# Groups of two tokens instead of four in a recurrence, with row statistics made one stage earlier

## The reference

```python
def step(h, bu_t):
    Wh = jnp.fft.ifft(lambdas * jnp.fft.fft(h)).real
    h_new = Wh + bu_t
    return (h_new, h_new)
...
y = jnp.einsum('sbn,dn->bsd', hs, C_w) + D * u
...
x = x + 0.5 * _L0_ffn_ref(_layernorm(x, axis=-1), L0_ffn_gate_w, L0_ffn_w1, L0_ffn_w2)
x = x + _L0_attn_ref(_layernorm(x, axis=-1), L0_attn_a_params, L0_attn_B_w, L0_attn_C_w, L0_attn_D)
x = x + 0.5 * _L0_ffn_ref(_layernorm(x, axis=-1), L0_ffn_gate_w, L0_ffn_w1, L0_ffn_w2)
```

## Time and profile before

| | us |
|---|---|
| median of 3 runs | 150.54 |
| lowest and highest run | 150.45, 153.68 |
| the profiled execution's own time | 150.5 |
| its span in the trace | 148.6 |
| PE busy | 128.5 (86%) |
| DVE busy | 88.2 (59%) |
| ACT busy | 56.1 (38%) |
| POOL busy | 56.0 (38%) |

### The profile page before, as it was taken

One profiled execution on the slowest core, in us unless ns is written; L12 is line 12 of the kernel. 1 busy time (PEld: TensorE's weight loads), 2 busy tenths in 40 slices (PEclk: granted clock), 3 DMA queues, 4 the chain that ended last, 5 costly groups with the idle time before them and its releaser, 6 DMA issues.

```text
span 148.6 us, 2493 instructions
## 1 busy us (share of the span) xinstructions
PE 128.5 (86%) x749; PEld 96.6 (65%) x749; DVE 88.2 (59%) x379; ACT 56.1 (38%) x156; POOL 56.0 (38%) x96
## 2 busy tenths in 40 slices
PE   5988989699799989379999999999989969999920
PEld 2315334289699965137887788778976249999810
DVE  1198787994467431257679668988894133755310
ACT  2522434235353302055756675752010035553200
POOL 3490002777205778001212211231100677665570
PEclk9999999999999999999999999999995599999995
DMA  4999995236660111690013441344024312211110
GB/s 89 305 351 401 350 290 144 55 108 185 194 203 22 57 53 53 213 321 35 2 45 101 146 133 39 123 148 146 0 76 158 91 46 56 56 38 40 43 45 18
DMA packets 15740, 18.49 MB, mean 124 GB/s; under 512 B 1904, under 2 KB 10608, under 8 KB 15600
## 3 DMA queue, kind: packets, MB, share of 16 engines
q1 hardware_dynamic: 13936, 15.34, 32.7%
q0 software_dynamic: 1280, 2.66, 6.3%
q10 hardware_dynamic: 512, 0.34, 0.9%
HBM read 12.70 MB, written 7.73 MB: 138 GB/s over the span
## 4 chain that ended last, share of the span: by engine, by line
PE 46%; DMA 14%; issue 10%; ACT 9%; POOL 7%; DVE 5%; SPq 4%; POOLq 1%
PE pair L1062 9%; PE pair L1075 9%; ACT u L520 7%; DMA w1s<-w 5%; PE pair L1158 5%; POOL xg L370 5%; PE pair L1149 4%; SPq L292 3%; PE pair L1180 3%; PE pair L1182 3%; PE pair L943 2%; DMA xg<-x,tok 2%; DMA x<-x_scratch 2%; DMA xg<-x_scratch,tok 2%; PE pair L1087 2%
## 5 line engine op out<-in xcount | busy, mean ns | idle before, releaser
L943 PE MATMUL pair<-warm_in,ones_bf 128*128 128x512 bf16 x61 | 18.9, 457 | 3.9 <-DMA x<-x_scratch 2.3
L1062 PE MATMUL pair<-xcT,w1s 128*128 128x160 f32 x128 | 20.5, 303 | 0.6 <-ACT xcT L452 0.6
L1062 PEld LDWEIGHTS pair<-xcT,w1s 128*128 128x128 f32 x128 | 18.0, 190 | 1.7 <-ACT xcT L452 1.7
L460 ACT ACTIVATE hT<-pair 128x320 f32<-128x320 f32 x32 | 13.8, 435 | 13.6 <-PE pair L1062 12.1
L1075 PE MATMUL pair<-hT,w2s 128*128 128x160 f32 x112 | 17.8, 302 | 0.0
L370 POOL DMA_INDIRECT xg<-x,tok x10 | 10.2, 1019 | 16.7 <-issue 16.7
L1075 PEld LDWEIGHTS pair<-hT,w2s 128*128 128x128 f32 x112 | 15.6, 190 | 0.0
L370 POOL DMA_INDIRECT xg<-x_scratch,tok x10 | 10.1, 1007 | 13.7 <-DMA x_scratch<-x 10.9
L943 PEld LDWEIGHTS pair<-warm_in,ones_bf 128*128 128x128 bf16 x61 | 6.8, 117 | 12.2 <-issue 4.1
L402 POOL TENSOR_TENSOR vb<-vq,st 128x128 f32<-128x128 f32 x8 | 3.8, 474 | 27.0 <-ACT vq L495 27.0
L381 POOL DMA_INDIRECT x_scratch<-xnew,tok x10 | 9.9, 985 | 10.3 <-DMA x_scratch<-x 7.6
(11 more groups left out here) (190 smaller groups left out, 242.8 us busy)
## 6 DMA issues: line engine op xcount, KB each, us to landing
x_scratch<-x SPq DMA_DIRECT2D x8, 272.0 KB, 2.1
...
```

Of the source, the lines that this page charges most:

```text
L460: nc.scalar.activation(hT[:, e % 2, half * HC:(half + 1) * HC, :], bank[4 + half][:, 0:HC * CAP] .rearrange("p (c s) -> p c s", c=HC), ACT ...
L943: M(bank[to][:, :], ones_bf[:, :], warm_in[:, :], start=True, stop=True)
L1062: ins = M(bank[4 + half][:, c * CAP:(c + 1) * CAP], w1s[:, i, ch * P:(ch + 1) * P], xcT[:, i * CAP:(i + 1) * CAP], start=True, stop=True)
```

## The change

- The recurrence works in groups of two tokens (`TR = 2`) and 256 groups a batch. `group_sums` becomes 2 matmuls of 256 columns that read `uT` with a stride; `vq`, `va`, `vb`, `z`, `zc`, `zs` are twice as wide; the part within a group becomes `within(i, 0)` and `within(i, 1)`, 2 matmuls and 432 columns each; the tables are smaller.
- POOL adds `state` for batches 0 to 6, DVE for batch 7.
- The mean and variance of `x`'s rows are made in the first expert stage. SP loads `x` into `x1` (`load_x`), DVE rates it (`rate_rows`, step `x`) into two more columns, and SP stores rows of 130 columns to `x1_scratch` (`store_x`). The rows of `xnew` are rated in step `o` as well, and a scatter waits for that. In the recurrence `stats` is gone, and `deviation` and `shift` are done for groups of batches (`RATED`).
- ACT's `normalise` is cut in halves on both sides of `turned_part`.
- The power levels 0 to 4 move from ahead of DVE's first gathered tile to between its steps `o`; levels 5 to 7 follow the last one.
- `x2` of batches 6 and 7 is added by PE and copied by ACT; `gate_back(6)` moves ahead of `carry(7)`. The `keep_warm` ahead of the recurrence has 10 matmuls instead of 14.

The core of the diff:

```diff
+    TR = 2
-    NG = SEQ // TB
+    NG = SEQ // TR
+    XP = D + 2
...
-        dve_steps = [steps("i0 i1 i2 i3 i4 d0 i5 i6 i7 i8 d1 i9 l0 f0 d2 "
-                         "o0 o1 d3 p5 o2 o3 d4 p6 o4 o5 d5 o6 d6 o7 o8 o9"),
+        dve_steps = [steps("i0 i1 i2 x0 i3 x1 i4 x2 d0 i5 x3 i6 x4 i7 x5 d1 i8 x6 i9 x7 l0 f0 d2 "
+                         "o0 o1 d3 p0 p1 o2 o3 d4 p2 p3 o4 o5 d5 p4 o6 d6 o7 o8 o9 p5 p6 p7"),
...
+            def load_x(b):
+                sp.dma_start(x1[:, b * TB:(b + 1) * TB, 0:D], tiles(x_rows, b)).then_inc(d_x1[b], 16)
+            def store_x(b):
+                sp.wait_ge(x_rated, b + 1)
+                sp.dma_start(tiles(x1_dram, b), x1[:, b * TB:(b + 1) * TB, :]).then_inc(d_fill, 16)
             for b in range(NB):
-                sp.wait_ge(d_gather[min(b + 3, NS - 1)], 16)
-                sp.dma_start(tiles(x1_dram, b), tiles(x_rows, b)).then_inc(d_fill, 16)
+                sp.wait_ge(d_gather[b], 16)
+                load_x(b)
+                if b >= 2:
+                    store_x(b - 2)
...
+                    if n == 0:
+                        pool.wait_ge(row_rated, j + 1)
...
+            def turn_forth(b):
+                pool.wait_ge(zs_r, b + 1)
+                pool.wait_ge(zc_r, b + 1)
+                if b >= 2:
+                    pool.wait_ge(y_ps, b - 1)
+                nc.gpsimd.tensor_tensor(state_out(b), by_group(zc), by_group(zs), ALU.add).then_inc(state_r, 1)
...
             for i in range(NB):
                 if i + 1 < NB:
                     copy_uT(i + 1)
+                if i == 1:
+                    deviation(3)
                 if i + 2 < NB:
-                    deviation(i + 2)
+                    normalise(i + 2, 0, TB // 2)
                 if i + 1 < NB:
                     turned_part(i + 1)
                 if i + 2 < NB:
-                    normalise(i + 2)
+                    normalise(i + 2, TB // 2, TB)
...
+                def rate_rows(b):
+                    dve.wait_ge(d_x1[b], 16)
+                    for t in range(b * TB, (b + 1) * TB):
+                        ins = V.bn_stats(sstat[:, t, :], x1[:, t, 0:D])
+                    link(ins)
+                    for t in range(b * TB, (b + 1) * TB):
+                        ins = V.bn_aggr(x1[:, t, D:XP], sstat[:, t, :])
+                    ins.then_inc(x_rated, 1)
...
+                        if n == 0:
+                            dve.wait_ge(row_sb, i + 1)
+                            link(V.bn_stats(nstat[:, i, :], xnew[:, i, 0:D]))
+                            V.bn_aggr(xnew[:, i, D:XP], nstat[:, i, :]).then_inc(row_rated, 1)
...
+                by_residue = uT[:, b % 2, :].rearrange("d (h r p) -> d r p h", h=2, r=TR)
+                for r in range(TR):
+                    ins = M(bank[5][:, 0:NG].rearrange("s (p h) -> s p h", h=2), vt[:, TR - 1 - r, :],
+                            by_residue[:, r, :, :], start=(r == 0), stop=(r == TR - 1))
...
+            def within(b, h):
+                if b >= 2 and h == 0:
+                    pe.wait_ge(x2_r, b - 1)
+                    pe.wait_ge(y_read, b - 1)
+                y = y_pair(b)
+                M(y[:, h, 0:TR * BLOCK], uT[:, b % 2, 2 * h * P:(2 * h + 1) * P], tab[:, :, :].rearrange("p r c -> p (r c)"),
+                  start=True, stop=False, skip_group_check=True)
+                ins = M(y[:, h, BLOCK:2 * BLOCK], uT[:, b % 2, (2 * h + 1) * P:(2 * h + 2) * P], tab[:, 0, :],
+                        start=False, stop=False, skip_group_check=True)
...
-            keep_warm(14, 7)
+            keep_warm(10, 7)
...
                 group_sums(i)
+                within(i, 0)
                 if i >= 1:
                     read_out(i - 1)
-                within_pairs(i)
                 turn_u(i + 1)
                 if i == NB // 2 + 2:
                     rank(1, 0)
-                within_rest(i)
+                within(i, 1)
```

More of the change, by code:

```diff
@@ L417, in _ @@
                 turn_cosine(i)
+                if i < LAST:
+                    turn_forth(i)
             gather(1)
@@ L860, in turn_forth @@
                     dve.wait_ge(y_ps, b - 1)
-                V.tensor_tensor(state[:, b % 2, :], zc[:, :], zs[:, :], ALU.add).then_inc(state_r, 1)
+                V.tensor_tensor(state_out(b), by_group(zc), by_group(zs), ALU.add).then_inc(state_r, 1)
             def add_back(b):
@@ L930, in _ @@
             encode_place(1, 1)
-            add_back(LAST - 1)
             index(1)
@@ L1233, in _ @@
                     rank(1, 0)
-                within_rest(i)
+                within(i, 1)
             group_sums(LAST)
+            within(LAST, 0)
             read_out(LAST - 1)
-            within_pairs(LAST)
             gates_within(LAST)
+            within(LAST, 1)
+            add_rows(LAST - 1)
             gates_carried(LAST)
-            within_rest(LAST)
             read_out(LAST)
```

265 lines of the change are left out of this document (123 added, 142 removed).

## The result

The changed kernel takes **163.1 us**, the median of 4 runs (160.74 to 163.43), beside 151.49 for the kernel before on the same chip (4 runs). The ratio is 1.071, 95% interval 1.045 to 1.096: slower, and outside the range given. The profiled execution of the changed kernel took 163.31 (span 161.4), that of before 150.5.

What follows compares the result with a forecast made beforehand. Bounds: PE and ACT taking turns in the recurrence, POOL's scatters in the first expert stage, then DVE there after the change. Sum: 150.5 + 2.6 (first stage) - 3.9 (recurrence) + 1.2 + 1.1 - 0.2 (end) = 151.3 us; range 148.3 to 155.5.

Steps and rivals of the forecast that it cites:

- the first expert stage: Gathers to last scatter: DVE becomes the bound through rating; last scatter starts at 60.6 instead of 57.15, 3.5 later.
- 4.7 late: Bound for the first expert stage if loads of x land 0.7 later each time (3.4) and DVE stalls once.
- Softmax to last scatter: First expert stage, from softmax start to the last scatter's start: 15.83 before, forecast 1.0 longer, with DVE the bound.
- less than DVE's own delay: First expert stage: g0 holds the third relu, so PE's fourth expert starts some 1.4 late, adding nothing to the sum.
- A fall of PE's clock in this stage: Sign of a wrong forecast: PE's granted clock falling in the first stage because of gaps between its steps o.
- over 90% busy from 31 to 60: Sign of a right forecast: DVE nearly full through the first expert stage.
- keep_warm: Ahead of turn_u(0): four fewer matmuls at 0.229 each give back 0.92.
- Recurrence: The seven gaps between turn_u starts shrink from 34.1 to 30.2, a gain of 3.9.
- The ring: Recurrence cycle over two batches: PE's within waits for gate_back of an earlier batch; 8.55 for two, 4.28 each.
- rival 3: Recurrence: group_sums' strided read of uT takes twice the time, +0.89 a batch, period 5.0, 156.3 us; chance 0.04.
- End of the recurrence: From turn_u(7) to the second stage's gather: +1.2 to va(7), +1.1 to gate_first, -0.2 before the gather.
- The slower rival: Over 153.5 us: doubled prices of wide operations give 154.5, late first-stage loads alone 152.5, both 155.7; chance 0.20.

Runs made afterwards that it cites:

- e3: The changed kernel with all eight loads of x issued at once ahead of the gathers, stores after them: 159.5 us, ratio 1.051.
- e11: The kernel before with only the change's loads and stores of x through SBUF, nothing rated: 153.9 us, ratio 1.011.
- e2: The kernel before with only the statistics and their traffic moved, groups of four, state on DVE: 159.0 us, ratio 1.055.
- e5: The changed kernel with group_sums reading uT in order and writing its sums strided: 160.9 us, ratio 1.065.
- e6: The changed kernel with the fourth expert's relu ahead of g0 in ACT's order: 158.7 us, ratio 1.050.
- e7: The changed kernel with 26 instead of 16 keep_warm matmuls ahead of the wait for the read back: 159.8 us, ratio 1.060.
- e12: The changed kernel with state added by DVE for every batch instead of by POOL: 160.3 us, ratio 1.055.
- e4: The changed kernel with power levels 0 to 4 again ahead of DVE's first gathered tile: 159.8 us, ratio 1.052.
- e9: The changed kernel with the edits of e3, e4, e5, e6 and e7 together: 155.2 us, ratio 1.020.
- e10: The kernel before with only x2 of batch 6 added by PE and copied by ACT: 151.2 us, ratio 1.000.
- e1: The changed kernel with the statistics, the traffic of x and the late power levels taken back: 162.8 us, ratio 1.078.

## Why the prediction was wrong, point by point

**The step that failed is the first expert stage**: "up to the softmax DVE has 8 x 1.19 + 7 x 0.42 + 2 copies of 0.25 = 12.9, and comes to `l0` at 43.8", with the third gather "near 27.80 + 2 x 1.3 = 30.4". Its prices were right (0.82 a step `o`, 0.75 to 0.82 a level against 0.87, 1.2 a batch), and so was the 12.9 of DVE's work (13.0 in e3); its mechanism, DVE bound by rating, was half of it. It took the transfers as free. What the runs show in its place: DVE starts that work at 32.16 and not at 30.4, and waits 2.9 for two loads in the middle of it, so the softmax starts at 48.42 (46.74 in the earliest execution of the same program) and not at 43.8. Of the late start 0.8 is a wrong reading: the earlier trace rows is the first gathered tile, the second comes 1.32 behind it, but the third lands at 31.24 in the kernel before already. In the profiles the added traffic alone moves the last scatter by 4.0 (e11), and with the rating by 7.2 (e2). The text did name late loads as a bound, "4.7 late" for the stage, with 0.7 more a load; they were 2 us more in the median (1.3 in e5, e6, e7 and e12) and 3.7 more for one. The 3.4 of the old copies, on the page of the kernel before, would have given that 0.7.

**Softmax to last scatter** was forecast 1.0 longer and is 2.7 longer. The moved levels, which were in the sum, cost 1.8 (e4); the lower clock, which was not, 1.3 (e6 and e3), and that is most of the 1.7 that are missing here. The two add up: e9, with both mended, needs 15.47, 3.1 less than the changed kernel and even less than before. The text said that ACT's `g0` would hold the `relu` and PE's fourth expert by 1.4, "less than DVE's own delay". The hold was right and 2.92 long, though only 0.62 to 1.11 in e5, e7 and e12, with the clock as low. A fall of PE's clock in this stage was named among what would make the prediction wrong, with no price in the sum or the range, and for gaps between the steps `o`; it came at 44.0, seven microseconds ahead of the first of them, behind PE's waits for gathered tiles. DVE, forecast over 90% busy from 31 to 60, was 76% busy.

**keep_warm**: -0.9 forecast, +1.1 measured for the stretch. "`keep_warm` ends after 2.3" holds at full clock (2.17 in e7 and e12); at the granted 0.50 it was 4.24. Here 2.0 of the 12 missing us lie, but they are not shown to be the change's: the same program took 2.17 in e12, and the kernel before's own fourteen took 4.68 to `turn_u(0)` in e10 where they had taken 3.27. The forecast had no term for either clock here.

**Recurrence**: -3.9 forecast, -1.0 measured; -1.45 at full clock (e6: gaps of 32.65). The ring was named rightly, and three terms were short. From `turn_u` to the end of the `vq` copies it is 3.46 (86.08 to 89.54) instead of 3.16, all `group_sums`. From there to the end of `gate_back` 3.96 (93.50) instead of 3.64: `zs` 1.29 instead of 1.08, and the two reads behind it 1.05 instead of 0.96; the scan ends where it was forecast. From there to `within` 0.15 instead of 0.05. That is 0.7 of the 0.76 in this pair; the last two pairs take 9.23 and 9.22. The first takes 9.82, and why it is 0.6 longer no run shows; the gap ahead of it is 4.82 instead of 4.1, of which the lower clock is 0.46 (4.36 in e6). "Nothing in the trace speaks for" the strided read: it came at 0.30, a third of what rival 3 had, and taking most of it back gave 0.8 (e5).

**End of the recurrence**: +2.1 forecast (with the -0.2), +2.85 measured. `va(7)` starts 114.93 - 109.49 = 5.4 after `turn_u(7)` instead of 4.8, and `gate_first` ends 4.44 after `va(7)` instead of 4.06; from there to the gather it is 0.45 shorter than before, where 0.2 was forecast. (In the kernel before the granted clock is not full up to the gather: it is 0.50 from 112 to 118.) The mechanism was right: DVE runs without a gap from batch 6's products through the second numbering to `va(7)`. Timeline of DVE:

```profile
111.70 0.69 DVE L912 TENSOR_TENSOR x<-pair,x 128x512 f32<-128x512 f32 x1
...
114.93 0.42 DVE L887 TENSOR_TENSOR va<-pair,ct 128x256 f32<-128x256 f32 x1
```

**What held**: POOL's prices and its add, which would cost 1.3 on DVE (e12); the groups of two costing the first stage nothing (e1). `x2` on PE, worth 0.2 in the forecast, is worth nothing in the kernel before (e10); in the changed kernel it was not tried alone. The slower rival had the doubled wide operations as its cause, which is not what happened on POOL (0.742 and 0.963); on DVE the scan is at its doubled price (0.69) and `zs` halfway (1.29 of 1.5); only its second half, late loads, was near, and its 155.7 is 7 us short. In sum, against the 12.0 that are missing in the profiled execution (163.3 - 151.3): start of the softmax 4.6, behind it 1.7, `keep_warm` 2.0, gaps 2.9, end 0.75. The first and the third differ from execution to execution: in e12 they are 2.9 and 0.1.

**What stays open**: which part of the 4.6 at the softmax is slower landing and which is SP's ring wasn't parted, since e3 breaks the ring and delays the gathers at once; what decides whether the clock falls ahead of `keep_warm`; and the rating of ten rows wasn't tried without the rating of `x`.
